# Edge steps of a graph network: low parts moved to VectorE, and the order of the four engines' work changed

## The reference, cut to what matters

```python
h = jnp.maximum(_layernorm(x), 0.0)
# layer 0: messages along edges, four aggregates for each receiver
m = jnp.concatenate([h[dst], h[src]], -1) @ W_pre.T + b_pre
mx, mn = segment_max(m, dst), segment_min(m, dst)      # 0 without edges
mean = segment_sum(m, dst) / deg_c
std = jnp.sqrt(relu(segment_sum(m * m, dst) / deg_c - mean * mean) + 1e-5)
agg = jnp.concatenate([mx, mn, mean, std], -1)
scaled = jnp.concatenate([agg, agg * amp, agg * att], -1)  # amp = log(deg_c + 1), att = 1 / amp
x = x + (jnp.concatenate([h, scaled], -1) @ W_post.T + b_post) @ W_lin.T + b_lin
# layer 1: mean of the edge attributes, then two dense layers
h = jnp.maximum(_layernorm(x), 0.0)
attr = segment_sum(edge_attr_128, dst) / jnp.maximum(counts, 1.0)
x = x + relu(jnp.concatenate([h, attr], -1) @ W1 + b1) @ W2 + b2
```

## Time and profile before

| | us |
|---|---|
| median of 3 timed runs | 1666.87 (1665.56 to 1671.47) |
| the profiled execution | 1669.48 |
| its span, first to last instruction | 1667.7 |
| busy in the span: PE, DVE, ACT, POOL | 1520.5, 1306.2, 930.2, 1293.9 |

### The profile page before, as it was taken

One profiled execution on the slowest core, in us unless ns is written; L12 is line 12 of the kernel. 1 busy time (PEld: TensorE's weight loads), 2 busy tenths in 40 slices (PEclk: granted clock), 3 DMA queues, 4 the chain that ended last, 5 costly groups with the idle time before them and its releaser, 6 DMA issues.

```text
span 1667.7 us, 33188 instructions
## 1 busy us (share of the span) xinstructions
PE 1520.5 (91%) x8747; PEld 1268.2 (76%) x8747; DVE 1306.2 (78%) x4229; ACT 930.2 (56%) x1976; POOL 1293.9 (78%) x1379
## 2 busy tenths in 40 slices
PE   2899999999999589999989999999999989999995
PEld 2789999999999468777777777777777777777783
DVE  5899999999999488777776677777777766777781
ACT  1799999999999334444434444444443444443441
POOL 1777777777778787888888888888888888888753
PEclk9799999999999889999999999999999999999998
DMA  3455555555555522233222233333233323333200
GB/s 85 163 208 206 205 205 203 201 201 202 204 204 190 171 86 83 82 85 82 85 78 80 82 89 88 90 91 87 87 89 81 83 85 91 91 91 92 82 20 17
DMA packets 158897, 197.94 MB, mean 119 GB/s; under 512 B 18912, under 2 KB 115321, under 8 KB 158858
## 3 DMA queue, kind: packets, MB, share of 16 engines
q1 hardware_dynamic: 136906, 149.93, 27.7%
q0 software_dynamic: 21952, 47.55, 9.5%
HBM read 111.11 MB, written 90.17 MB: 121 GB/s over the span
## 4 chain that ended last, share of the span: by engine, by line
PE 43%; POOL 27%; issue 16%; DVE 8%; ACT 2%; another core or an unknown queue 2%; POOLq 1%; DMA 1%; SPq 0%; DVEq 0%; ACTq 0%
PE bank L571 12%; POOL y L474 6%; PE bank L580 5%; POOL rows L461 5%; POOL agg_lo L400 5%; POOL hs L461 5%; PE bank L592 3%; PE bank L590 3%; PE bank L591 3%; PE bank L554 3%; PE bank L562 3%; PE bank L620 2%; POOL attr_mean L486 2%; POOL xdc L413 2%; PE bank L617 2%
## 5 line engine op out<-in xcount | busy, mean ns | idle before, releaser
L617 PE MATMUL bank<-comb_hi,agg_lo 128*128 128x384 f32 x588 | 212.6, 362 | 67.7 <-POOL agg_lo L400 64.8
L461 POOL DMA_INDIRECT hs<-table,idx x196 | 202.6, 1034 | 59.7 <-issue 56.9
L461 POOL DMA_INDIRECT rows<-table,idx x196 | 200.5, 1023 | 59.7 <-issue 59.7
L613 PE MATMUL bank<-comb_lo,agg_hi 128*128 128x384 f32 x588 | 230.5, 392 | 16.5 <-DVE nout L983 12.6
L474 POOL DMA_INDIRECT y<-nout,oidx x196 | 196.1, 1001 | 54.8 <-issue 51.6
L379 POOL TENSOR_TENSOR runs<-nx,b_all 128x512 f32<-128x512 f32 x98 | 125.6, 1282 | 109.0 <-DVE nx L993 108.9
L571 PE MATMUL bank<-w_sb,nut 128*128 128x128 f32 x1568 | 201.5, 282 | 3.9 <-ACT nut L780 2.8
L614 PE MATMUL bank<-comb_hi,agg_hi 128*128 128x384 f32 x588 | 201.1, 342 | 0.0
L571 PEld LDWEIGHTS bank<-w_sb,nut 128*128 128x128 f32 x1568 | 183.4, 192 | 22.5 <-issue 11.8
L617 PEld LDWEIGHTS bank<-comb_hi,agg_lo 128*128 128x128 f32 x588 | 112.9, 192 | 92.9 <-POOL agg_lo L400 86.6
L620 PE MATMUL bank<-comb_sd,agg_sd 128*128 128x384 f32 x392 | 170.4, 518 | 0.0
(11 more groups left out here) (180 smaller groups left out, 4159.4 us busy)
## 6 DMA issues: line engine op xcount, KB each, us to landing
table<-rows SPq DMA_DIRECT2D x98, 512.0 KB, 2.7
rows<-in_x SPq DMA_DIRECT2D x98, 256.0 KB, 3.1
y<-nout SPq DMA_DIRECT2D x98, 256.0 KB
inv<-inv_row SPq DMA_DIRECT2D x49, 256.0 KB
attr<-in_edge_attr SPq DMA_DIRECT2D x48, 256.0 KB
keep<-keep_row SPq DMA_DIRECT2D x49, 128.0 KB
reset<-reset_row SPq DMA_DIRECT2D x49, 128.0 KB
lift<-lift_row SPq DMA_DIRECT2D x49, 128.0 KB
```

The lines of the kernel that those rows point to most:

```text
L461: pool.indirect_dma_start(out=to[:, s, j, :], out_offset=None, in_=of, in_offset=bass.IndirectOffsetOnAxis(ap=idx[:, s, which, j:j + 1], a ...
L613: pe.matmul(acc[:, 0:SCALERS * P], hi, w_lo, start=(a == MX), stop=False, skip_group_check=True)
L617: pe.matmul(acc[:, 0:SCALERS * P], lo, w_hi, start=False, stop=False, skip_group_check=True)
```

## The change

- DVE makes the low parts of maximum and minimum too (`low_part` on DVE with an additional wait on e_layer0); POOL makes none.
- POOL's step is now: scatter(k-2), receiver_part(k+1), attr_to_mean(k), gather(k+4). The scatter gets a small addition of its own, scatter_go, ahead of its DMAs.
- PE's step: turn_sender(k+1), layer0 first quarter, sender_part(k+1), turn_receiver(k+1), second quarter, turn_normed(k-1), third quarter, turn_attr(k), hidden(k-1), fourth quarter, outputs(k-1).
- ACT: message ahead of receiver_turned and normalise, message_squared behind; the three high parts and the mean's square ahead of both hidden parts, the deviation last.
- DVE: first mix, three scans and the mean, receiver_low, normed_low, second mix, squares to variance, the attribute scan, low parts of maximum and minimum, third mix, low part of the mean, fourth mix, moments.
- Instructions are otherwise the same. Some waits are added that follow from the order (message on e_max and e_min, sender_part on e_b).

The core of the diff:

```diff
+            def scatter(c, i):
+                pool.wait_ge(fixed, 1)
+                pool.wait_ge(sem("e_out"), c + 1 + EU * i)
...
+                pool.tensor_copy(oidx[:, c % 4].rearrange("p (r h) -> p r h", h=2), index[:, 2, t, :]).then_inc(sem("e_oidx"), 1)
+                pool.wait_ge(sem("e_oidx"), c + 1 + EU * i)
+                pool.tensor_tensor(scatter_go[:], eps_col[:], eps_col[:], ALU.add)
+                for j in range(TILES):
+                    pool.indirect_dma_start(
...
             def edge_step(k, i):
...
+                if edge(k - 2):
+                    scatter(k - 2, i)
+                if edge(k + 1):
+                    receiver_part(k + 1, i)
+                if edge(k):
+                    attr_to_mean(k, i)
+                if edge(k + 4):
+                    gather(k + 4, i)
```

```diff
             def edge_step(k, i):
...
+                have, ahead, behind = edge(k), edge(k + 1), edge(k - 1)
+                if ahead:
+                    turn_sender(k + 1, i)
+                if have:
+                    pe.wait_ge(sem("e_hdl"), k + 1 + EU * i)
+                    layer0(k, 0, i)
+                if ahead:
+                    sender_part(k + 1, i)
+                    turn_receiver(k + 1, i)
+                if have:
+                    layer0(k, 1, i)
+                if behind:
+                    turn_normed(k - 1, i, not ahead)
+                if have:
+                    layer0(k, 2, i)
+                    turn_attr(k, i)
+                if behind:
+                    hidden(k - 1, i)
+                if have:
+                    layer0(k, 3, i)
+                if behind:
+                    outputs(k - 1, i)
```

```diff
+                ahead, behind = edge(k + 1), edge(k - 1)
+                if ahead:
+                    sender_turned(k + 1, i)
+                if behind:
+                    spread(k - 1, i)
+                if ahead:
+                    message(k + 1, i)
+                    receiver_turned(k + 1, i)
+                if behind:
+                    normalise(k - 1, i)
+                if ahead:
+                    message_squared(k + 1, i)
+                if behind:
+                    normed_turned(k - 1, i)
+                if ahead:
+                    high_part(MX, "e_max", run_max[:, (k + 1) % 2, :], k + 1, i)
+                    high_part(MN, "e_min", run_min[:, (k + 1) % 2, :], k + 1, i)
+                    mean_squared(k + 1, i)
+                    high_part(ME, "e_mean_b", mean_b[:], k + 1, i)
+                if behind:
+                    hidden(0, 7, k - 1, i)
+                    hidden(1, 1, k - 1, i)
+                if ahead:
+                    deviation(k + 1, i)
```

```diff
             def low_part(a, rows, c, i):
 
                 dve.wait_ge(sem(f"e_hi{a}"), c + 1 + EU * i)
+                if c >= 2:
+                    dve.wait_ge(sem("e_layer0"), TILES * (c - 1) + TILES * EU * i)
                 dve.tensor_tensor(agg_lo[:, c % 2, a, :], rows, agg_hi[:, c % 2, a, :],
                                   ALU.subtract).then_inc(sem(f"e_lo{a}"), 1)
...
                 have, ahead, behind = edge(k), edge(k + 1), edge(k - 1)
                 if edge(k - 2):
+                    outputs(k - 2, i)
                 if behind:
+                    factors(k - 1, i)
+                if have:
+                    mix(k, 0, i)
+                if ahead:
+                    scan_max(k + 1, i)
+                    scan_min(k + 1, i)
+                    scan_sum(k + 1, i)
+                    message_mean(k + 1, i)
+                    receiver_low(k + 1, i)
                 if behind:
+                    normed_low(k - 1, i)
+                if have:
+                    mix(k, 1, i)
                 if ahead:
+                    scan_squares(k + 1, i)
+                    square_mean(k + 1, i)
+                    variance(k + 1, i)
                 if have:
+                    scan_attr(k, i)
+                if ahead:
+                    low_part(MX, run_max[:, (k + 1) % 2, :], k + 1, i)
+                    low_part(MN, run_min[:, (k + 1) % 2, :], k + 1, i)
                 if have:
+                    mix(k, 2, i)
                 if ahead:
                     low_part(ME, mean_b[:], k + 1, i)
                 if have:
+                    mix(k, 3, i)
+                    moments(k, i)
```

More of the change, by code:

```diff
@@ new lines, in turn_attr @@
+            def turn_attr(c, i):
+                pe.wait_ge(sem(f"e_attr_in{c % 2}"),
+                           16 * (c // 2 + 1) + 8 * EU * i + (16 if c == EDGE_CHUNKS - 1 else 0))
+                if c == 0:
+                    pe.wait_ge(sem("n_h2l"), NODE_CHUNKS)
+                if c >= 1:
+                    pe.wait_ge(sem("e_attr_run"), c + EU * i)
+                for j in range(TILES):
+                    mm = pe.transpose(bank[2][:, j * P:(j + 1) * P], attr[:, c % 2, j, :], ident[:])
+                mm.then_inc(sem("e_turned_attr"), 1)
@@ new lines, in sender_part, with turn_normed @@
+            def sender_part(c, i):
+                pe.wait_ge(sem("e_hst"), c + 1 + EU * i)
+                if c >= 1:
+                    pe.wait_ge(sem("e_b"), c + EU * i)
+                    pe.wait_ge(sem("e_bsq"), c + EU * i)
+                pe.matmul(bank[3][:], ws_t[:], hst[:, c % 2, :], start=True, stop=True).then_inc(sem("e_b_psum"), 1)
+            def turn_normed(c, i, last):
+                pe.wait_ge(sem("e_norm2"), c + 1 + EU * i)
+                if last and c >= 1:
+                    pe.wait_ge(sem("e_h2l"), c + EU * i)
+                for j in range(TILES):
+                    mm = pe.transpose(bank[0][:, j * P:(j + 1) * P], h2[:, c % 2, j, :], ident[:])
+                mm.then_inc(sem("e_turned2"), 1)
@@ L1192, in edge_step @@
-                if have:
-                    mix_amp(k, 2, i)
+                    scan_attr(k, i)
+                if ahead:
+                    low_part(MX, run_max[:, (k + 1) % 2, :], k + 1, i)
+                    low_part(MN, run_min[:, (k + 1) % 2, :], k + 1, i)
+                if have:
+                    mix(k, 2, i)
                 if ahead:
```

605 lines of the change are left out of this document (273 added, 332 removed).

## The result

| set of runs, each on one chip | before, us | changed, us | ratio, 95% interval | profiled runs |
|---|---|---|---|---|
| first | 1668.13 | 2000.04 | 1.1994 (1.1969 to 1.2019) | completions late |
| chip 13 (a0, b0, e5) | 1666.37 | 1606.96 | 0.9639 (0.9623 to 0.9655) | at once |
| chip 8 (a1, e6, e7, e8) | 1667.61 | 2003.39 | 1.2022 (1.2000 to 1.2044) | late |
| chip 11 (a2, e1b, e3b, e9) | 1666.21 | 1606.18 | 0.9641 (0.9621 to 0.9660) | at once |

The same kernel is 20% slower than before in two sets and 3.6% faster in two others, while the kernel before moves by 0.1%. Forecast were 1592 us and a range of 1553 to 1655. The measurement that the prediction was made for is the first: 2000 us, outside the range and on the other side.

What follows compares the result with a forecast made beforehand. GpSimd was taken to bound at 21.91 us a step; less 2.51 for low parts, plus 0.6 go and 0.2 sharing, 20.2. Over 41 steps 70 us, plus some 5 from slack, were saved: 1592 us, range 1553 to 1655.

Steps and rivals of the forecast that it cites:

- (a): GpSimd: the low parts leave it, taking 2.51 us off each step, from 21.91 to 19.40 us.
- (c): VectorE: the low parts arrive, two more subtractions of 1.38 us a step; it then needs 19.2 us.
- (d): GpSimd and VectorE sharing SBUF access: longer GpSimd instructions, +0.2 us a step net, making GpSimd 20.2 us.
- floor rival: Sharing costs nothing and TensorE's 19.15 us step bounds: 113 us less, 1553.8 us; chance 0.20.
- (b): GpSimd: a second go instruction for the scatter adds 0.6 us a step, making 20.0 us.
- (e): TensorE's new order: no instruction changes, each wait looks met, all costed at nothing.
- e_b near 5.0: Sender's message: product at 3.8 us from the step's start, so e_b ready near 5.0 us.
- (f): GpSimd's queue: attribute scan late, mean behind receiver_part, gather last; 7 us of slack, costed at nothing.
- no visible difference: Rival: the new order, some wait late by 2 us, loses about GpSimd's gain; 1660 to 1675 us, chance 0.07.
- The blocked VectorE: Rival: a two-SBUF-input VectorE instruction loses up to 3.1 us a step behind GpSimd's run; 1683 us, chance 0.09.
- no wait for GpSimd's agg_lo: Sign that the forecast is right: TensorE's L617 no longer waits for GpSimd's low parts.
- wrong altogether if TensorE waits long at a new place: Sign of a wholly wrong forecast: a long new TensorE wait, hidden or sender_part being first to look at.

Runs made afterwards that it cites:

- a0: The changed kernel, unaltered, on chip 13: 1606.96 us.
- b0: The kernel before, unaltered, traced on chip 13: 1665.9 us.
- e5: The changed kernel with turn_normed on TensorE behind the third quarter of layer 0 instead of ahead of it: 1629.49 us.
- a1: The changed kernel, unaltered, on chip 8: 2003.39 us.
- e6: The changed kernel with the mean's low part right behind the two others, ahead of the third quarter's mixes: 1989.14 us on chip 8.
- e7: The changed kernel with GpSimd's order of before (receiver part, gather, scatter, attribute mean), without the low parts and the second go: 1602.10 us.
- e8: The kernel before with all three low parts on VectorE and GpSimd's order of the changed kernel: 1656.24 us on chip 8.
- a2: The changed kernel, unaltered, on chip 11: 1606.18 us.
- e1b: The changed kernel with ScalarE's normalise ahead of message and receiver_turned, run again on chip 11: 1626.84 us.
- e3b: The kernel before with all three low parts on VectorE and no order changed, run again on chip 11: 1540.28 us.
- e9: The changed kernel without three quarters of the scatters and of the gathers behind the first four chunks; most edge output isn't written: 1530.00 us.
- e3c: The kernel before with all three low parts on VectorE and no order changed, run a third time, on chip 3: 1651.75 us.
- e3: The kernel before with all three low parts on VectorE and no order changed, on chip 2: 1538.78 us.
- e4: The changed kernel with the low parts of maximum and minimum back on GpSimd behind receiver_part, new order kept: 1691.03 us.

## Why the prediction failed, point by point

- **What bounds the kernel before**: right. 21.91 us a step against TensorE's 19.15, and GpSimd the cause. e3b's step of 19.15 is the floor that the earlier trace rows gave.
- **(a) and (c), the low parts**: right in direction and too small. Alone they bring 127 us where completions are at once; I had 75 for the whole change. The second go is the order's, not theirs, and the added sharing that I charged in (d) hardly occurs with them alone: the mean's low part takes 739 ns in e3b. My floor rival, 1553.8 us, had this mechanism; the step is right, and the remaining 14 us I have not taken apart. VectorE's need of 19.2 us was too high as well: it is busy 525.89 us in 600, 16.8 a step.
- **(d), sharing**: the step that failed where completions are at once. I took 0.2 us net. VectorE's mean low part pays 3.17 us, the amount of the earlier trace rows, which I had as a rival with 0.09, and had put beside a VectorE need that was 2 us too high. GpSimd pays 4 x (1.17 - 1.00) = 0.7 us for the scatters and 0.5 for the index copy (0.656 us, against 0.19 in e3b and e7), and gets 0.3 back on the gathers. The new go takes 0.82 where (b) took 0.6, but the old one falls from 0.62 to 0.19, so the two together cost 0.5 with the new wait. From 19.4 us after (a) that gives the measured 20.7 us a step. This step and its 1607 us lie in my forecast's 19.7 to 20.8 and 1567 to 1613, but half by luck: GpSimd is full as foretold, VectorE is too, and PE waits for VectorE where I had seen slack of 1.7 us.
  The Trainium skill, page "SBUF — State Buffer", section "Who interferes with whom", has the mutual exclusion and says that issue order decides who is blocked. The trace agrees on the exclusion, with 3.86 us beside a busy GpSimd and 0.68 us in e9. On the order it doesn't, if one goes by the starts in the profile: VectorE's instruction begins at 1001.93, GpSimd's xdc at 1002.57, and VectorE's is the one that is held. My own reason for the 0.2, that with two low parts fewer GpSimd's runs get shorter, failed with the new order: it set four other instructions in a row, 3.3 us.
- **(e), TensorE's order costed at nothing**: held where completions are at once (e9 reaches the floor with it). Not in the first set: "e_b near 5.0" was 7 us late, and turn_normed, costed at nothing like the rest, stood 7.2 us a step and held h2l, and with it the attribute scan, in 24 of 37 steps. The sentence that should have stopped me is my own, on the earlier trace rows and the "remote" of the earlier trace rows: that ScalarE and VectorE there learn late of finished transposes. I put it down to PE's stand before L617 and expected it to go with the stand. b0 refutes that: the same stand, and nobody late. I then used ends of matmuls as the times at which others go on, in a trace that showed 2.4 to 3.1 us between the two.
- **(f), attribute scan late, gathers behind the mean**: the step that failed in the first set. I checked that receiver_part had 7 us of slack and costed the rest at nothing. I didn't ask what a late scan does to the twelve DMAs queued behind it, when those DMAs in turn fall together with late completions that the scan's own inputs need. e7 undoes GpSimd's part of this step (and the second go with it) and takes 401 of the 2003 us away.
- **The rivals**: "no visible difference" named a PE queue that waits and then holds everyone, but from lateness of 2 us and with 0.07. The blocked VectorE ended slower only through the wrong sum. None of them had a loop.
- **The signs foretold**: no wait for GpSimd's agg_lo, right; "wrong altogether if TensorE waits long at a new place", right in kind, at turn_normed rather than at hidden or sender_part.

What stays open: why completions are late in some sets. Seven sets ran on different chips, as far as their numbers are known (the first one's isn't); three are late in every traced kernel, four in none. Whether it is the chip or the time isn't decided. The following was only found, not tested: leaving aside e_layer0, whose events are partly missing (some others lack a few, and e7 lacks nearly all of e_turned2), completions that end while GpSimd is in a run of indirect DMAs are late far more often.

```
                       ends outside a run       ends inside a run
                       at once   late(>0.3 us)  at once   late
changed, first set       104       6              18       83
changed, chip 8          108       5              12       84
e8, chip 8                69      13              67      114
e3c, chip 3               96      13              53      105
```

It doesn't hold everywhere: in the kernel before, 44 of 81 are late outside and 103 of 173 inside, and in e7 all 39 outside, which end just behind a run, against 61 of 189 inside; and in the at-once sets the same runs make nothing late. The same traces have one regularity more: in the kernel before, all 37 receiver transposes are told between 1.4 and 2.0 us behind the end of the run of eight gathers, in e7 all 39 about 1.0 us behind the end of the run of twelve, and in the first set's trace of the changed kernel 1.4 us behind it in the median. e9 was meant to test the connection. The recording isn't the cause: the three executions of the first set without the profiler took 1994 to 2009 us. That completions really are told late, and the matmuls don't end late behind modelled ends, is likely, not shown. For it: in the kernel before, four groups with ends over 1.3 us apart (e_out_psum to e_turned_attr) are told one behind the other between 1038.30 and 1038.47, and in the changed kernel PE keeps starting matmuls at its usual pace while the completion is out. The Trainium skill, page "Perfetto Trace Analysis", section "Tensor Engine Instruction (MATMUL, LD_WEIGHTS)", says that PE's end is estimated from an instruction's size, with the write's acknowledgement and the semaphore's propagation behind it; it gives no duration. Here it is 0.01 us in one kind of set and up to 9 us in the other.

## What to carry to other kernels

Move the work first and measure it alone: e3 has all of the gain, and beats both kernels in both kinds of set (1539 and 1652 us), while an order rewritten in the same stroke hid it. In an order written by hand, look behind every wait that is moved for the long queue that now depends on it, here twelve DMAs behind a scan made late; a step with slack in every wait can still close into a loop when signals come late. And a "remote" wait whose producer had long ended is a warning that the schedule's times cannot be read off the producers' ends.

## What the runs showed of the hardware

- TensorE's completions reached other engines 0.01 us after the matmul in four sets, and in three sets often late, in every kernel traced there: by 6 to 8 us in the median for two completions of the changed kernel, by 2.4 to 3.1 us for four of the kernel before, by about 1 us in e7. What this costs differs with the kernel: nothing before (GpSimd-bound, 1666 and 1668 us), 112 us with the low parts alone, 396 us with the whole change.
- A VectorE instruction with two SBUF inputs that meets a back-to-back run of GpSimd instructions can be held for the whole run, not for one of them: 3.86 us instead of 0.69 beside four instructions of together 3.3 us. Even one of 128x4 elements took 3.2 us in e4.
- Moving the blocked instruction ahead in its queue did not free it: it was blocked again (3.39 us), and GpSimd's run began 0.3 us behind its start as it had 0.6 us behind before. I read this as two engines that lock in phase; no run tests that by itself.
